# Attention with ones beside the values: one product per head, division through 32x32 turns on VectorE, and token normalising moved to ScalarE

## What is computed

```python
x = x + tanh(g_xattn[0]) * L0_xattn(layernorm(x), ctx, ctx)
x = x + tanh(g_ffn[0])   * L0_ffn(layernorm(x))
x = x + tanh(g_xattn[1]) * L1_xattn(layernorm(x), ctx, ctx, mask)
x = x + tanh(g_ffn[1])   * L1_ffn(layernorm(x))

def xattn(q, k, v):                    # 16 heads of 16 features
    q, k, v = heads(q @ Wq.T + bq), heads(k @ Wk.T + bk), heads(v @ Wv.T + bv)
    s = -0.25 * q @ k.T                # first layer
    s = where(mask, min, rope(q) @ rope(k).T)   # second layer
    return merge(softmax(s) @ v) @ Wp.T + bp
```

## Time and profile before

| | |
|---|---|
| three executions, median | 755.70, 760.03, 771.83 us; 760.03 us |
| the profiled execution | 764.37 us |
| its span in the profile | 762.60 us |
| mean granted clock of TensorE | 0.968 |
| TensorE busy | 670.9 us, 88% of the span |
| VectorE busy | 60% |
| ScalarE busy | 46% |
| POOL busy | 30% |
| first scores of block 0, block 7 | at 32.4, 121.0 us |
| first scores of block 8, block 15 | at 364.7, 457.2 us |
| output product of block 15 | at 472.3 us |

### The profile page before, as it was taken

The page is one execution under the profiler, slowest core; times in us unless marked ns, Lnnn a source line. Parts: engine busy times, 40 slices in busy tenths (PEclk is TensorE's granted clock), DMA queues, the critical chain, the costliest instruction groups (busy, mean ns, idle before and its releaser), DMA issues.

```text
span 762.6 us, 13653 instructions
## 1 busy us (share of the span) xinstructions
PE 670.9 (88%) x5072; PEld 542.0 (71%) x5072; DVE 456.3 (60%) x919; ACT 348.5 (46%) x776; POOL 226.6 (30%) x213
## 2 busy tenths in 40 slices
PE   5799988989997867874898987999988999999998
PEld 4567765768885545552555544999976899999997
DVE  3767754511106566768688655456897877777713
ACT  2456564656663232132555645323247555566400
POOL 5744411400000230035756221000134454445500
PEclk9999997999999998997999999999999999999999
DMA  6955761391000033205767740400000566655313
GB/s 237 276 154 149 208 177 37 125 425 44 0 0 2 2 141 127 51 1 125 131 130 144 127 99 5 163 1 1 1 1 1 180 210 220 218 208 198 119 28 110
DMA packets 61349, 87.20 MB, mean 114 GB/s; under 512 B 17256, under 2 KB 50664, under 8 KB 60264
## 3 DMA queue, kind: packets, MB, share of 16 engines
q1 hardware_dynamic: 60496, 85.90, 38.0%
q10 hardware_dynamic: 800, 0.59, 0.3%
HBM read 63.54 MB, written 18.73 MB: 108 GB/s over the span
## 4 chain that ended last, share of the span: by engine, by line
PE 70%; DVE 13%; issue 8%; ACT 3%; DMA 3%; POOL 3%; ACTq 0%; SPq 0%; DVEq 0%; POOLq 0%
PE ps L1036 68%; DVE keep L1951 2%; DMA keep<-in_x 1%; DVE mcol L1766 1%; PE ps L1042 1%; DVE keep L1962 1%; DMA att<-in_wd 1%; DVE keep L1959 1%; DVE keep L1944 1%; DVE G L2163 1%; DVE mcol L1768 1%; ACT vp L744 1%; ACT big L744 1%; DVE hhi_s L2090 1%; POOL tlo L674 1%
## 5 line engine op out<-in xcount | busy, mean ns | idle before, releaser
L1036 PE MATMUL ps<-thi,whi 128*128 128x256 f32 x256 | 73.6, 288 | 4.9 <-POOL tlo L674 2.1
L1036 PE MATMUL ps<-keep 128*128 128x120 bf16 (+7 forms) x473 | 59.7, 256 | 20.4 <-DVE keep L1951 15.3
L1036 PE MATMUL ps<-thi,wlo 128*128 128x256 f32 x256 | 72.4, 283 | 0.0
L1036 PE MATMUL ps<-tlo,whi 128*128 128x256 f32 x256 | 72.4, 283 | 0.0
L840 ACT ACTIVATE ps<-ps 128x256 f32<-128x256 f32 x128 | 47.6, 372 | 38.5 <-PE ps L1036 38.5
L1036 PEld LDWEIGHTS ps<-keep 128*128 128x128 bf16 (+1 forms) x473 | 34.6, 113 | 40.7 <-DVE keep L1951 26.3
L946 ACT ACTIVATE att<-ps 128x512 f32<-128x512 f32 x48 | 28.6, 596 | 67.5 <-PE ps L1036 67.4
L545 POOL TENSOR_TENSOR kbr<-khi,keep 128x616 fp32r<-128x616 f32 x32 | 39.9, 1270 | 63.9 <-PE ps L1036 60.4
L1036 PEld LDWEIGHTS ps<-thi,whi 128*128 128x128 f32 x256 | 49.0, 191 | 6.8 <-issue 4.7
L1036 PE MATMUL ps<-xhi,phi 128*128 128x512 f32 x128 | 50.7, 396 | 2.8 <-ACT ps L840 2.8
L744 ACT ACTIVATE big<-ps 77x512 f32<-77x512 f32 x64 | 34.5, 588 | 36.5 <-PE ps L1036 35.9
(11 more groups left out here) (236 smaller groups left out, 1856.4 us busy)
## 6 DMA issues: line engine op xcount, KB each, us to landing
...
```

Of the source, the lines that this page charges most:

```text
L1036: return pe.matmul(out, lhsT, rhs, start=start, stop=stop, skip_group_check=True)
```

## The change

Five parts.

1. `Vpad` is filled with 1.0 where it was filled with 0.0, and the values of every head stand in its columns 0 to 15, so the columns 16 to 31 are ones. `weigh_values` has one product per head: 8 products of 256 columns in place of 16. Strip j of the bank holds for head 2j+a, in columns 256a to 256a+255, the 16 features in its upper partitions and 16 equal rows of the denominator below them. `par` isn't used there any more.
2. `divide` on VectorE transposes 32x32 blocks of the whole bank (128x512) into SBUF (`turned`), so that tokens stand in the partitions and one column of each block is the denominator. It takes the maximum of these 128x16 denominators with a tiny number (`den`), the reciprocal (`rec`), multiplies the features by the reciprocal broadcast over 16 columns (`scaled`, 128x256), and transposes 32x32 blocks back into `attnT`. Each of the five waits for the one before. The next `weigh_values` of the bank waits for the first transpose (`turn_done`); `project_out` and `scale_rows` wait for the last (`attn_done`), as before.
3. `invert` on ScalarE goes, and with it its logarithm and exponential.
4. `normalise(n)` for blocks 4 to 7 and every `normalise_second(k)` go from VectorE to ScalarE, as x times the inverse deviation plus a bias. `normalise` of blocks 0 to 3 stays on VectorE. On ScalarE they stand ahead of the last exponentials of a round, `normalise_second` one round later than it stood on VectorE; those of blocks 7 and 15 stand inside the stages that follow the attentions.
5. POOL forms that bias, minus the mean times the inverse deviation: two more small operations per call.

```diff
             def inv_std(n):
+                scalar = B // 2 <= n < B
+                steps = n + 2 * min(max(n - B // 2, 0), B // 2)
                 pool.wait_ge(mv_done, n * 2 + 2)
                 pool.tensor_tensor(veps[:, n % 2], mv[:, n % 2, :, 1], eps, ALU.add).then_inc(veps_done, 1)
-                pool.wait_ge(veps_done, n + 1)
+                if scalar:
+                    pool.tensor_tensor(nmean[:, n % 2], mv[:, n % 2, :, 0], minus, ALU.mult).then_inc(veps_done, 1)
+                pool.wait_ge(veps_done, steps + 1 + scalar)
                 if 2 <= n < B + 2:
                     pool.wait_ge(xn_done, 2 * n - 2)
-                pool.tensor_tensor(rstd[:, n % 2], veps[:, n % 2], mhalf, ALU.pow).then_inc(rstd_done, 1)
+                pool.tensor_tensor(rstd[:, n % 2], veps[:, n % 2], mhalf, ALU.pow
+                                   ).then_inc(veps_done if scalar else rstd_done, 1)
+                if scalar:
+                    pool.wait_ge(veps_done, steps + 3)
+                    pool.tensor_tensor(nbias[:, n % 2], nmean[:, n % 2], rstd[:, n % 2], ALU.mult).then_inc(rstd_done, 1)
...
                 pool.tensor_tensor(fveps, fmv[:, tiles(b), 1], eps, ALU.add).then_inc(fveps_done, 1)
-                pool.wait_ge(fveps_done, k + 1)
-                pool.tensor_tensor(frstd[:, tiles(b)], fveps, mhalf, ALU.pow).then_inc(frstd_done, 1)
+                pool.tensor_tensor(fnmean, fmv[:, tiles(b), 0], minus, ALU.mult).then_inc(fveps_done, 1)
+                pool.wait_ge(fveps_done, 3 * k + 2)
+                pool.tensor_tensor(frstd[:, tiles(b)], fveps, mhalf, ALU.pow).then_inc(fveps_done, 1)
+                pool.wait_ge(fveps_done, 3 * k + 3)
+                pool.tensor_tensor(fnbias[:, tiles(b)], fnmean, frstd[:, tiles(b)], ALU.mult).then_inc(frstd_done, 1)
...
                 pool.wait_ge(v_raw, unit + 1)
-                v2 = Vpad[0:SK, 2 * j:2 * j + 2].rearrange("p b (h a) m -> p b h a m", a=2)
-                for a in range(2):
-                    part = v2[:, :, :, a, HD * a:HD * a + HD]
-                    ins = pool.tensor_tensor(part, part, bv[0:SK].rearrange("p (h a m) -> p h a m", a=2, m=HD)[:, :, a, :]
-                                             .unsqueeze(1).to_broadcast([SK, 2, PAIRS, HD]), ALU.add)
-                ins.then_inc(v_done, 1)
-
-            pool.memset(Vpad.rearrange("p b h m -> p (b h m)"), 0.0).then_inc(cleared, 1)
+                part = Vpad[0:SK, 2 * j:2 * j + 2, :, 0:HD]
+                pool.tensor_tensor(part, part, bv[0:SK].rearrange("p (h m) -> p h m", m=HD)
+                                   .unsqueeze(1).to_broadcast([SK, 2, H, HD]), ALU.add).then_inc(v_done, 1)
+
+            pool.memset(Vpad.rearrange("p b h m -> p (b h m)"), 1.0).then_inc(cleared, 1)
...
-            def invert(n, c):
-
-                r = rden[:, S * c:S * c + S]
-                act.wait_ge(pv_ps, 2 * n + c + 1)
-                if n > 0:
-                    act.wait_ge(attn_done, 2 * n + c - 1)
-                act.activation(r, ps[:, PV_BANK + c, S:2 * S], ACT.Ln, bias=tiny[:, 0:1]).then_inc(ln_done, 1)
-                act.wait_ge(ln_done, 2 * n + c + 1)
-                act.activation(r, r, ACT.Exp, scale=-1.0).then_inc(rden_done, 1)
+            def normalise(n):
...
+                    act.activation(xn[:, n % 2, t, :], x_sb[:, n * 2 + t, :], ACT.Identity, bias=nbias[:, n % 2, t:t + 1],
+                                   scale=rstd[:, n % 2, t:t + 1]).then_inc(xn_done, 1)
+
+            def normalise_second(k):
+                b = k % B
+                out = xn2[:, k % 2] if k < B else xn_all[:, 2 * b:2 * b + 2, :]
+                act.wait_ge(frstd_done, k + 1)
+                if 2 <= k < B:
+                    act.wait_ge(xt2_ps, k - 1)
+                for t in range(2):
+                    at = 2 * b + t
+                    act.activation(out[:, t, :], x_sb[:, at, :], ACT.Identity, bias=fnbias[:, at:at + 1],
+                                   scale=frstd[:, at:at + 1]).then_inc(xn2_done, 1)
 
             def attend(layer):
...
-                    if n > lo:
-                        invert(n - 1, 1)
                     exponentials(n, (0, 1))
...
                     if n + 3 < hi and layer == 1:
                         raw_queries(n + 3)
-                    if layer == 1:
-                        invert(n, 0)
+                    if n + 4 < hi and layer == 0:
+                        normalise(n + 4)
+                    if n - 2 >= lo:
+                        normalise_second(n - 2)
                     exponentials(n, (6, 7))
-                    if layer == 0:
-                        invert(n, 0)
                     if n + 3 < hi and layer == 0:
                         copy_xt(n + 3)
...
                         round_shared(2)
+                    if n == hi - 1:
+                        normalise_second(n - 1)
...
                 layer, b = divmod(n, B)
                 if b > 0:
-                    pe.wait_ge(attn_done, 2 * n + c - 1)
+                    pe.wait_ge(turn_done, 2 * n + c - 1)
                 elif c == 0:
                     pe.wait_ge(mT_done, n + 2)
...
-                for den in range(2):
-                    for a in range(2):
-                        for j in range(4):
-                            h = 8 * c + 2 * j + a
-                            lhsT = par[0:SK, a, :] if den else Vpad[0:SK, b, h, :]
-                            ins = mm(ps[32 * j:32 * j + 32, PV_BANK + c, S * den:S * den + S], lhsT,
-                                     PT[layer][0:SK, h, :], a == 0, a == 1)
+                for a in range(2):
+                    for j in range(4):
+                        h = 8 * c + 2 * j + a
+                        ins = mm(ps[32 * j:32 * j + 32, PV_BANK + c, S * a:S * a + S], Vpad[0:SK, b, h, :],
+                                 PT[layer][0:SK, h, :])
                 ins.then_inc(pv_ps, 1)
...
@@ -1658,7 +1676,7 @@
                     dve.wait_ge(x_rest_in, 16)
                 if n >= B:
                     dve.wait_ge(x2_done, b + 1)
-                if n >= B + 2:
+                if n >= 2:
                     dve.wait_ge(rstd_done, n - 1)
...
-            def normalise_second(k):
-                b = k % B
...
             def divide(n, c):
-                dve.wait_ge(rden_done, 2 * n + c + 1)
+                i = 2 * n + c
+                dve.wait_ge(pv_ps, i + 1)
+                dve.transpose(turned, ps[:, PV_BANK + c, :]).then_inc(turn_done, 1)
+                dve.wait_ge(turn_done, i + 1)
+                dve.tensor_scalar(den, turned4[:, :, :, HD], TINY, None, ALU.max).then_inc(div_step, 1)
+                dve.wait_ge(div_step, 3 * i + 1)
+                dve.reciprocal(rec, den).then_inc(div_step, 1)
+                dve.wait_ge(div_step, 3 * i + 2)
+                dve.tensor_tensor(scaled.rearrange("p (t a d) -> p a t d", a=2, d=HD), turned4[:, :, :, 0:HD],
+                                  rec.unsqueeze(3).to_broadcast([P, 2, S // 32, HD]), ALU.mult).then_inc(div_step, 1)
+                dve.wait_ge(div_step, 3 * i + 3)
                 if n > 0:
                     dve.wait_ge(proj_ps, n)
-                dve.tensor_tensor(attnT[:, c, :], ps[:, PV_BANK + c, 0:S], rden[:, S * c:S * c + S], ALU.mult
-                                  ).then_inc(attn_done, 1)
+                dve.transpose(attnT[:, c, :], scaled).then_inc(attn_done, 1)
...
                         maxima(n + 2, 0)
-                    if n + 4 < B:
-                        normalise(n + 4)
                     if n > 0:
...
                     divide(n, 0)
-                    if n > 0:
-                        normalise_second(n - 1)
```

44 lines of the change are left out of this document (20 added, 24 removed).

## The result

| | before | changed |
|---|---|---|
| median | 762.70 us (4 executions, 755.70 to 771.83) | 777.13 us (4 executions, 775.99 to 782.46) |
| ratio, 95% interval | | 1.0223 [1.0175, 1.0271] |
| span of the profiled execution | 762.6 us | 774.0 us |
| granted clock, mean over the span | 0.968 | 0.938 |

The account below looks back on a forecast made before the run. TensorE was taken to set steady blocks, VectorE 2 us behind. First attention -4.3, second +0.2 and slow clock +7.3 gave +3.2 us on a profiled 764.4, scaled to the median: 763 us; range 748 to 782.

Parts of the forecast that it names:

- rival C: VectorE's divisions: slow transposes, 2.75 us per division, 0.7 us more for 26 of 32, +18 us to 781; chance 0.20.
- Price of a division: VectorE's five dependent instructions per group: 2.05 us, 1.7 us more than the 0.34 replaced; transposes about 0.69 and 0.42.
- Rivals B: Both attentions: division costs 1.2 us or less, so TensorE's saving comes through, together -22 us, 738; chance 0.13.
- capped at 5.8 + 0.4 = 6.2 us: First attention, start of block 7: a chain of DMAs limits the gain to 6.2 us, whatever TensorE and VectorE do.
- 4.96 + 1.7 = 6.66: Second attention: VectorE's stretch from first maxima to TensorE's start grows to 6.66 us; period 14.65 us, +0.95 a block.
- The clock: Second attention: TensorE gaps of about 3.4 us halve its clock, some 1.45 us on the path, five gaps, +7.3 us.
- Rival A: Second attention: TensorE's clock stays up, so the forecast without the 7.3 us, about 756 us; chance 0.17.
- Block 14 takes 11.2 ... I take 14 at 8.8: End of the second attention: block 14 falls from 11.2 to 8.8 us, -2.4; the maxima's DMA allows no less.
- 15 at -0.5, since both late divisions stand on VectorE's list: Last block of the second attention, 15.1 us before: only 0.5 us less, as VectorE's list holds both late divisions.
- block 8, where no division precedes, -0.5: First block of the second attention: 0.5 us shorter, since no division precedes it.
- it has 5 us free per block, so this costs nothing: ScalarE takes over normalising, two to four instructions of about 0.50 us per block, at no cost.
- 26 of 32 divisions on the path: Both attentions: added division time counts for 26 of 32 divisions, all but those hidden in the DMA-bound blocks.

Follow-up runs that it names:

- experiment 7: Changed kernel with the 1 MB load of output weights moved from round 4 of SyncE's queue to behind the first attention: 772.94 us, ratio 1.0122.
- experiment 3: Changed kernel plus 10 unread bf16 filler products in TensorE's gap ahead of the second attention's turned maxima: 775.62 us, ratio 1.0169; longer first version 799.80 us.
- experiment 8: Changed kernel without the 128x4 copy ending the second statistics, aggregates written straight to their final place: 772.99 us, ratio 1.0152.
- experiment 1: Changed kernel with the second maxima ahead of the first division on VectorE's list in the second attention: 767.72 us, ratio 1.0047.
- experiment 4: Kernel before with only the normalising moved to ScalarE and the bias on POOL: 768.71 us, ratio 1.0060.
- experiment 6: Changed kernel with the first transpose of each of the 32 divisions run twice, 0.74 us more each: 803.32 us (two executions), ratio 1.0534.

## Why the prediction was right, and where it wasn't

It said 763 us in a range of 748 to 782; the time is 777, inside it, with the forecast on the right side of zero and too small: +3.2 on the profiled execution became +11.4. That the range holds 777 is in part luck: its upper end was the 781 of rival C, slow transposes, and C's mechanism wasn't there. The forecast had given 0.66 to a difference of less than 2%; the ratio lies at 2.2%.

- **Price of a division: right.** 2.06 us against 2.05. Transposes took 702 to 708 and 445 ns against 0.69 and 0.42; the maximum, the reciprocal and the multiplication 0.21, 0.25 and 0.42 to 0.47. The forecast took the Trainium skill's one price (VectorE: DVE Perf Modes, The three transpose paths), 311 ns for a 128x128 bf16 transpose, to mean that a transpose costs about what another operation of its width does; that holds here for 32-bit data from PSUM. Rivals B and C fall with these rows.
- **First attention: right in its blocks and in what caps it; the cap was put too high.** Blocks 2 and 3 took 11.45 and 11.79 us against 11.6, and the cap by the chain of DMAs was shown by experiment 7. But of the -5.41 at block 7's scores 1.76 lie ahead of block 0, so the change brought 3.65 us there, and not the 6.2 of the step "capped at 5.8 + 0.4 = 6.2 us". The step took the chain to be as long as before; it took 1.9 us more (experiment 7). The near hit of -5.41 is luck. Block 7 itself grew by 2.06 us against 1.95.
- **Second attention, VectorE's stretch: right in place; the period 0.4 us short.** The step "4.96 + 1.7 = 6.66" measured 6.56, 6.92 and 6.73 in blocks 9 to 11, and 7.2 at full clock (experiment 3). The period without the clock was 15.1, not 14.65. The missing part is POOL: 4.96 held a copy of 0.67 already, and it took up to 0.93 and, at full clock, 1.2, because it waits for POOL's addition. Without it one block at clock 1.00 came to 14.28 us (experiment 8).
- **The clock: right in kind, 1.1 instead of 1.45 a block.** The gaps were 3.09 to 3.45 us in rounds 9 to 11 and 2.7 in 12 and 13, against 3.4. Rival A falls: granted clock 0.81 to 0.94 in blocks 9 to 13. The sum for these blocks, +10.85 against +11.72, is closer than its parts, which err in opposite ways: 3.6 without the clock and 7.25 for it were forecast, and experiment 3 shows 6.3 and 5.4. What I had counted wrong is their number. The last such gap, 2.70 us at 454.92, stands ahead of block 14, so it is six and not five: block 14 ran at 0.70 and took 10.48 us. This is one failed part of the step "Block 14 takes 11.2 ... I take 14 at 8.8". The other is its floor, "the maxima's DMA allows no less": in experiment 1 block 14 ran at clock 1.00 and still took 10.1 us, and block 15 began after a wait of 1.53 us for that DMA.
- **The end: wrong.** "15 at -0.5, since both late divisions stand on VectorE's list" came out at +2.13. Each division there stands behind a weight split of 1.2 us, and TensorE waits 4.27 us ahead of the last output product, which then runs at half speed, 3.78 us instead of 1.99; the second row is of the kernel before:

```profile
482.33 3.78 PE L1056 MATMUL ps<-att,big 128*128 128x256 f32 x8 [4.27 <-DVE big L1793]
```

```profile
472.32 1.99 PE L1036 MATMUL ps<-att,big 128*128 128x256 f32 x8 [0.91 <-DVE big L1775]
```

- **Block 8: wrong by 1.1 us.** "block 8, where no division precedes, -0.5": but its own first division stands between its maxima, with a gap of 3.05 us behind it.
- **"it has 5 us free per block, so this costs nothing", of ScalarE: right for steady blocks, wrong for the two last ones** (experiment 4), where an instruction ahead of the exponentials is on the path.
- **26 of 32 divisions on the path: not refuted, perhaps low.** Doubling a transpose cost 24 to 26 us, which is all 32 at 0.74; 26 of them are 19, inside the interval of two executions (experiment 6).
- **A slip in the range.** Its lower end takes 0.4 us for 18 divisions, where rival C takes 26 for the same; with 26 it would be 746 instead of 749.

The profiles' +11.4 is less than the ratio's 17 us because of the executions that were profiled: before, 764.37 us, 4.3 over its median of 760.03, and after, 775.99, the lowest of four. Not settled: in which stages these 5 us lie. The pattern and expert stages scatter by 3 to 7 us from one execution to the next in kernels that are alike there.
